# Local attention: order of maxima, exponentials and roots, the rotary halves in one operation, and the band mask on VectorE

## The chip, the cores and the metric

The kernel runs on one core of one Trainium2 chip. The metric is the device time of one launch in microseconds (us), as the median of several runs. Engines are named as in the profile: PE is TensorE (PEld its weight loads), DVE is VectorE, ACT is ScalarE, POOL is GpSimd, SP is SyncE.

## The reference, cut to what matters

The program is a four-layer decoder: each layer has an attention, a cross attention and a feed-forward part, each followed by a layer norm. Everything is f32, with a batch of 4 sequences of 512 tokens and a width of 128. The change lies in the feed-forward part of layer 1, which is itself a transformer of `DEPTH` = 6 blocks. Each block is a local attention and a gated feed-forward. Of the local attention, these lines of the reference tell what is computed (16 heads of 64, a window of 32):

```python
q = l2norm(q) * qs
k = l2norm(k) * ksc
...
q = q * cos * scale + rotate_half(q) * sin * scale
inv = 1.0 / scale
k = k * cos * inv + rotate_half(k) * sin * inv
out = local_attention(q, k, v)
...
mask = (it < jb) | (it > jb + w) | (jb == -1)
sim = jnp.einsum('bhwie,bhwje->bhwij', bq, bk2) * QK_SCALE
sim = jnp.where(mask, -jnp.finfo(sim.dtype).max, sim)
attn = jax.nn.softmax(sim, -1)
out = jnp.einsum('bhwij,bhwje->bhwie', attn, bv2)
```

`l2norm` divides a head's 64 values by the root of the sum of their squares; `rotate_half` swaps the two halves of 32 values of each head, with a sign. A query sees itself and the 32 keys before it. The kernel adds a band that is 0 where a key is seen and -1e30 elsewhere.

## The kernel before, in words

`local_transformer` (L2364) runs six blocks in a hardware loop; each calls `local_attention` (L1902) and then `gelu_ffn`. All weights of a block are loaded a block ahead.

`local_attention` cuts the 4 x 512 tokens into 16 tiles of 128 and each tile into four units of work, so G = 64. Each engine has its own program, all written over the same steps s = -7 ... 68, and each runs strictly in that order; semaphores tie them together. A step holds work of several ages:

- the query or key part of unit n = s + 7 (`LEAD`): PE projects 512 columns (L2010), ACT squares them (`local_squares`, L2092), DVE sums the squares of each head (`local_norm`, L2180), ACT makes the inverse roots by a logarithm and an exponential (L2114, L2117: "the roots"), and DVE multiplies the projection, still in its PSUM bank, by them into `local_raw` (L2190);
- POOL's rotary embedding of unit n (L2146 to L2152): `raw * cos`, the two swapped halves times `sin` in two operations, and their sum into `local_rot`;
- the transposition of unit s + 4 by PE (L2039), copied by ACT into `local_Q` or `local_K` (L2101, L2107);
- in two of four steps a value projection (L2046), copied out by DVE (L2202);
- the scores. PE makes those of two units at once, in the even steps (L2021, L2028), into three PSUM banks in turn. For each unit, DVE takes the row maxima (`local_negmax`, L2184), ACT the exponentials with their sums, four instructions (L2123), and DVE the reciprocal (L2205) and the probabilities (`local_probs`, L2208);
- of the unit before, PE's transposition of the probabilities (L2055) and ACT's copy of it (L2131); of the unit before that, PE's product with the values (L2068), copied out in even steps (L2167). Once in a tile PE does the output projection (L2077), and DVE adds it to the tokens (L2173).

The projections of queries, keys, values and output share **two PSUM banks**, used in turn in the order of `uses`: within the four steps of a tile qk0, v, qk1, v, qk2, qk3, out. PE waits before each projection until the one two places back has been read (`wait_for_bank`, L1992): for a query or key projection this is `scaled`, which L2190 raises. So qk1, qk2 and the next tile's qk0 each wait for the `local_raw` of the step before, and qk3 for a value copy.

The band mask is added by PE: before the scores of a pair, one matmul for each of the two banks multiplies a bf16 unit matrix with a bf16 band (`m.unit`, `m.bands`, L2020 to L2022), and the scores accumulate on it. `local_transformer` makes both tables once (L2383 to L2386).

The functions as they stand:

## Time and profile before

| what | value |
|---|---|
| median of 3 runs | 5413.22 us (5384.35 to 5419.07) |
| the profiled execution | 5386.55 us, its span 5384.8 us |
| busy share of the span | PE 84%, DVE 56%, ACT 54%, POOL 37% |
| POOL, rotary: L2149, L2146, L2152 | 557.6, 488.2 and 486.7 us busy |
| exponentials, L2123 | 474.2 us and 309.8 us for their sums |

The six passes of the local attention lie between 1262 and 3396 us. Each is a few us of start, a lead-in of seven steps in which only queries, keys and values are made, 64 steps with scores, and a drain. In the even part of a pass the pattern repeats from tile to tile, so that one tile tells what a pass costs. A share of busy time over the whole span says little here, since other stages have other limits.

### The profile page before, as it was taken

Reading aid. Unit: us, or ns where it says so; the run is one execution under the profiler, and the core shown is the slowest. Engines: PE = TensorE matmul, PEld = TensorE weight load, DVE = VectorE, ACT = ScalarE, POOL = GpSimd, SP = SyncE. Lnnn points to the kernel's source line nnn. Section 1 sums busy time; section 2 is a strip of 40 time slices with the busy share of each in tenths; the row PEclk is TensorE's granted clock in tenths of the full one; section 3 lists DMA queues with packets and bytes.
Section 4 is the critical chain, followed back from the end, with each engine's and each line's share of the span. In section 5 each row is a group of like instructions: output and inputs, shape, how many; then the busy total and the mean of one; then the engine's idle time right before and its main releaser. Section 6 shows DMA issues by size and latency. Waiting matters only on the chain. (4 is left out here: it accounts for less than half of the span.)

```text
span 5384.8 us, 98536 instructions
## 1 busy us (share of the span) xinstructions
PE 4535.6 (84%) x35524; PEld 2696.3 (50%) x35524; DVE 3041.0 (56%) x5774; ACT 2904.6 (54%) x8810; POOL 1985.9 (37%) x2126
## 2 busy tenths in 40 slices
PE   6998699997998979979889889855658988888999
PEld 2663355564654645646646556424445653223343
DVE  6551354455756747647557567359984554653333
ACT  4543334455756747747657577467764442553322
POOL 1320000236948939849569398013321310000000
PEclk8999789899999989999999999866669997996689
DMA  1000000001111111111111111100000000001000
GB/s 56 2 1 4 17 12 5 18 2 28 47 40 41 45 39 45 44 39 47 46 33 47 40 44 43 43 0 1 1 1 11 2 4 7 9 5 34 4 0 8
DMA packets 34474, 122.85 MB, mean 23 GB/s; under 512 B 8484, under 2 KB 9512, under 8 KB 32296
## 3 DMA queue, kind: packets, MB, share of 16 engines
q1 hardware_dynamic: 33960, 116.23, 8.0%
q8 instruction: 294, 4.82, 0.4%
q14 instruction: 220, 1.80, 0.1%
HBM read 37.24 MB, written 1.05 MB: 7 GB/s over the span
## 5 line engine op out<-in xcount | busy, mean ns | idle before, releaser
L706 POOL MEMSET norm_eps<- 128x1 f32 x16 | 1.6, 98 | 1596.4 <-POOLq L116 1551.9
L2149 POOL TENSOR_TENSOR local_other<-local_raw,local_sin 128x256 f32<-128x256 f32 x768 | 557.6, 726 | 60.2
L2010 PE MATMUL ps<-arena,local_xs 128*128 128x512 f32 x768 | 437.5, 654 | 111.2 <-DVE local_raw L2190 61.1
L2146 POOL TENSOR_TENSOR local_rot<-local_raw,local_cos 128x512 f32<-128x512 f32 x384 | 488.2, 1271 | 67.9 <-DVE local_raw L2190 67.9
L2152 POOL TENSOR_TENSOR local_rot<-local_rot,local_other 128x512 f32<-128x512 f32 x384 | 486.7, 1268 | 30.1
L2123 ACT ACTIVATE ps<-ps,local_negmax 128x96 f32<-128x96 f32 x1536 | 474.2, 309 | 41.5 <-DVE local_negmax L2184 41.4
L2190 DVE SCALAR_TENSOR_TENSOR local_raw<-local_inverse,ps 128x512 f32<-128x512 f32 x384 | 264.0, 687 | 278.3 <-ACT local_inverse L2117 278.3
L2180 DVE TENSOR_REDUCE local_norm<-local_squares 128x8 f32<-128x512 f32 x384 | 263.0, 685 | 129.5 <-ACT local_squares L2092 129.5
L2092 ACT ACTIVATE local_squares<-ps 128x512 f32<-128x512 f32 x384 | 229.8, 598 | 155.2 <-PE ps L2010 155.0
L2123 ACT ACTIVATION_READ_ACCUMULATOR ps<-ps,local_negmax 128x1 f32 x1536 | 309.8, 202 | 0.0
L2055 PE MATMUL ps<-const,local_probs 128*96 128x128 f32 x1536 | 239.7, 279 | 77.3 <-DVE local_probs L2208 77.3
L2039 PE MATMUL ps<-const,local_rot 128*128 128x128 f32 x1536 | 245.3, 282 | 50.5 <-POOL local_rot L2152 50.5
L2055 PEld LDWEIGHTS ps<-const,local_probs 128*96 128x96 f32 x1536 | 173.2, 127 | 194.2 <-DVE local_probs L2208 102.2
L2039 PEld LDWEIGHTS ps<-const,local_rot 128*128 128x128 f32 x1536 | 173.9, 141 | 191.8 <-POOL local_rot L2152 99.1
L2068 PE MATMUL ps<-local_pts,local_V_span 96*64 96x64 f32 x6144 | 266.9, 230 | 0.5
L2068 PEld LDWEIGHTS ps<-local_pts,local_V_span 96*64 96x64 f32 x6144 | 213.4, 139 | 72.2 <-issue 71.0
L2131 ACT COPY local_pts<-ps 96x512 f32<-96x512 f32 x384 | 221.4, 577 | 22.2 <-PE ps L2055 22.2
L2101 ACT ACTIVATE local_Q<-ps 128x512 f32<-128x512 f32 x192 | 114.6, 597 | 218.6 <-PE ps L2039 218.6
L1486 DVE TENSOR_REDUCE l3a_limits<-ps 128x1 f32<-128x512 f32 x256 | 165.0, 686 | 114.0 <-PE ps L1334 114.0
L2208 DVE TENSOR_TENSOR local_probs<-ps,local_total 128x384 f32<-128x384 f32 x384 | 214.1, 558 | 14.6 <-DVE local_total L2205 1.5
L2184 DVE TENSOR_REDUCE local_negmax<-ps 128x4 f32<-128x384 f32 x384 | 210.3, 548 | 7.0 <-PE ps L2028 7.0
L2010 PEld LDWEIGHTS ps<-arena,local_xs 128*128 128x128 f32 x768 | 120.0, 196 | 181.3 <-DVE local_raw L2190 104.1
(519 smaller groups left out, 10843.7 us busy)
## 6 DMA issues: line engine op xcount, KB each, us to landing
local_V_span<-local_V SPq DMA_DIRECT2D x96, 384.0 KB, 4.0
local_V_span<-local_V SPq DMA_DIRECT2D x96, 256.0 KB, 3.6
arena<-in_L1f_a SPq DMA_DIRECT2D x7, 2176.0 KB, 8.5
local_V_span<-local_V SPq DMA_DIRECT2D x72, 128.0 KB, 2.3
arena<-in_L3f SPq DMA_DIRECT2D x1, 3460.0 KB, 11.2
arena<-in_L1f_f SPq DMA_DIRECT2D x6, 537.5 KB, 3.9
arena<-in_L0f SPq DMA_DIRECT2D x1, 2824.5 KB, 9.7
arena<-in_L0x SPq DMA_DIRECT2D x1, 2049.5 KB, 9.3
```

Of the source, the lines that this page charges most:

```text
L2010: nc.tensor.matmul(bank("qk", n)[:, :], tokens_of(tile), w("Wqkv", QKV[i] * 512, (QKV[i] + 1) * 512), start=True, stop=True)\
L2039: mm = nc.tensor.transpose(TURN[:, c * P:(c + 1) * P], m.rot[:, n % 4, c * P:(c + 1) * P], core.ident)
L2055: mm = nc.tensor.transpose(PT[0:SPAN, u * P:(u + 1) * P], m.probs[:, g % 2, u, :], core.ident)
L2068: mm = nc.tensor.matmul(OUT[DH * h:DH * h + DH, c * SPAN_Q:(c + 1) * SPAN_Q], m.V_span[:, tile % 2, half_span, (2 * c + h) * DH:(2 * c + h ...
L2092: nc.scalar.activation(m.squares[:, n % 2, :], bank("qk", n)[:, :], ACT.Square).then_inc(squared, 1)
L2123: nc.scalar.activation(scores, scores, ACT.Exp, bias=m.negmax[:, s % 2, u:u + 1], accum_out=m.total[:, s % 2, u:u + 1])\
L2131: nc.scalar.copy(m.pts[:, g % 3, :, :].rearrange("p u q -> p (u q)"), PT[0:SPAN, :])\
L2146: link(nc.gpsimd.tensor_tensor(rot, raw, m.cos[:, t, a * DH:(a + 1) * DH].unsqueeze(1) .broadcast_to([P, 8, DH]), ALU.mult))
L2149: link(nc.gpsimd.tensor_tensor(other[:, :, lo:lo + HALF], raw[:, :, HALF - lo:DH - lo], m.sin[:, t, a * DH + lo:a * DH + lo + HALF].unsque ...
L2152: nc.gpsimd.tensor_tensor(rot, rot, other, ALU.add).then_inc(rotated, 1)
L2180: nc.vector.tensor_reduce(m.norm[:, n % 4, :], heads(m.squares[:, n % 2, :]), AX_X, ALU.add)\
L2190: nc.vector.scalar_tensor_tensor(out=heads(m.raw[:, n % 4, :]), in0=m.inverse[:, n % 4, :].unsqueeze(2).broadcast_to([P, 8, DH]), scalar=1 ...
```

## The change

Four things, all in the local attention:

- PE no longer adds the band. DVE adds it to the scores in their PSUM bank, one operation of 128 x 384 for each unit, and waits for it before the maxima. The two bf16 tables and their making go.
- On DVE, the maxima come ahead of the squares' sums, and the scaling into `local_raw` moves from before the exponentials' wait to the end of the step, behind the probabilities.
- On ACT, the four exponentials of a unit come ahead of the roots.
- On POOL, the two half-width products with `sin` become one of full width that reads the halves swapped.

```diff
@@ -1893,8 +1893,6 @@
         self.negmax, self.total = tmp("negmax", [P, 2, 4]), tmp("total", [P, 2, 4])
         self.probs, self.pts = tmp("probs", [P, 2, 4, SPAN]), tmp("pts", [SPAN, 3, 4, P])
         self.oT = tmp("oT", [P, 2, CHUNKS, TILE])
-        self.unit = tmp("unit", [P, P], BF16)
-        self.bands = tmp("bands", [P, 2, 4, SPAN], BF16)
         self.eps = tmp("eps", [P, 1])
         self.tiny = tmp("tiny", [P, 1])
 
@@ -1959,6 +1957,9 @@
 
     def heads(a):
         return a.rearrange("p (h d) -> p h d", d=DH)
+
+    def halves(a):
+        return a.rearrange("p (h j f) -> p h j f", j=2, f=HALF)
 
     with core.stage() as st:
         xs_low, xs_high = st.sem("xs_low"), st.sem("xs_high")
@@ -2016,10 +2017,6 @@
                     if s >= 2:
                         pe.wait_ge(probs_ready, s - 1)
                     first = tile % QT * TILE + SPAN_Q * half_span
-                    edge = int(tile % QT == 0 and half_span == 0)
-                    for i in range(2):
-                        nc.tensor.matmul(SC[(s + i) % 3][:, 0:UNITS * SPAN], m.unit[:, :],
-                                         m.bands[:, edge, :, :].rearrange("p u k -> p (u k)"), start=True, stop=False)
                     for u in range(UNITS):
                         for h in range(2):
                             for i in range(2):
@@ -2027,8 +2024,7 @@
                                 rows = slice(DH * h, DH * h + DH)
                                 mm = nc.tensor.matmul(SC[(s + i) % 3][rows_of(h, i), u * SPAN:(u + 1) * SPAN],
                                                       m.Q[rows, tile % 2, c, SPAN_Q * half_span:SPAN_Q * (half_span + 1)],
-                                                      m.K[rows, c, first:first + SPAN], start=False,
-                                                      stop=(u == UNITS - 1))
+                                                      m.K[rows, c, first:first + SPAN], start=True, stop=True)
                     mm.then_inc(scores_ready, 1)
                 n = s + LEAD - TURN_LAG
                 if 0 <= n < G:
@@ -2106,6 +2102,13 @@
                             act.wait_ge(scores_ready, 2 * (tile - 2))
                         nc.scalar.copy(m.K[:, c:c + 4, WINDOW + t * TILE:WINDOW + (t + 1) * TILE],
                                        TURN[:, :].rearrange("p (c q) -> p c q", c=4)).then_inc(flip_read, 1)
+                if 0 <= s < G:
+                    act.wait_ge(max_ready, s + 1)
+                    for u in range(UNITS):
+                        scores = SC[s % 3][:, u * SPAN:(u + 1) * SPAN]
+                        nc.scalar.activation(scores, scores, ACT.Exp, bias=m.negmax[:, s % 2, u:u + 1],
+                                             accum_out=m.total[:, s % 2, u:u + 1])\
+                          .then_inc(exp_ready, 1)
                 n = s + LEAD
                 if n < G:
                     act.wait_ge(summed, n + 1)
@@ -2116,13 +2119,6 @@
                     act.wait_ge(log_ready, n + 1)
                     nc.scalar.activation(m.inverse[:, n % 4, :], m.log[:, n % 4, :], ACT.Exp, scale=-0.5)\
                       .then_inc(inverted, 1)
-                if 0 <= s < G:
-                    act.wait_ge(max_ready, s + 1)
-                    for u in range(UNITS):
-                        scores = SC[s % 3][:, u * SPAN:(u + 1) * SPAN]
-                        nc.scalar.activation(scores, scores, ACT.Exp, bias=m.negmax[:, s % 2, u:u + 1],
-                                             accum_out=m.total[:, s % 2, u:u + 1])\
-                          .then_inc(exp_ready, 1)
                 g = s - 1
                 if 0 <= g < G:
                     act.wait_ge(turned, g + 1)
@@ -2145,10 +2141,9 @@
                     pool.wait_ge(flipped, n - 3)
                 link(nc.gpsimd.tensor_tensor(rot, raw, m.cos[:, t, a * DH:(a + 1) * DH].unsqueeze(1)
                                              .broadcast_to([P, 8, DH]), ALU.mult))
-                for lo in (0, HALF):
-                    link(nc.gpsimd.tensor_tensor(other[:, :, lo:lo + HALF], raw[:, :, HALF - lo:DH - lo],
-                                                 m.sin[:, t, a * DH + lo:a * DH + lo + HALF].unsqueeze(1)
-                                                 .broadcast_to([P, 8, HALF]), ALU.mult))
+                link(nc.gpsimd.tensor_tensor(halves(m.other[:, :]), halves(m.raw[:, n % 4, :])[:, :, ::-1, :],
+                                             m.sin[:, t, a * DH:(a + 1) * DH].rearrange("p (j f) -> p j f", f=HALF)
+                                             .unsqueeze(1).broadcast_to([P, 8, 2, HALF]), ALU.mult))
                 nc.gpsimd.tensor_tensor(rot, rot, other, ALU.add).then_inc(rotated, 1)
 
         @st.block.vector
@@ -2172,6 +2167,13 @@
                     dve.wait_ge(projected, tile + 1)
                     nc.vector.tensor_tensor(place_x, bank("out", tile)[:, 0:TILE], place_x, ALU.add)\
                       .then_inc(x_done, 1)
+                if 0 <= s < G:
+                    dve.wait_ge(scores_ready, s // 2 + 1)
+                    tile, half_span, _ = place(s)
+                    band = core.c("band_first" if tile % QT == 0 and half_span == 0 else "band")
+                    link(nc.vector.tensor_tensor(sc, sc, band.unsqueeze(1).broadcast_to([P, UNITS, SPAN]), ALU.add))
+                    nc.vector.tensor_reduce(m.negmax[:, s % 2, :], sc, AX_X, ALU.max, negate=True)\
+                      .then_inc(max_ready, 1)
                 n = s + LEAD
                 if n < G:
                     dve.wait_ge(squared, n + 1)
@@ -2179,18 +2181,6 @@
                         dve.wait_ge(inverted, n - 3)
                     nc.vector.tensor_reduce(m.norm[:, n % 4, :], heads(m.squares[:, n % 2, :]), AX_X, ALU.add)\
                       .then_inc(summed, 1)
-                if 0 <= s < G:
-                    dve.wait_ge(scores_ready, s // 2 + 1)
-                    nc.vector.tensor_reduce(m.negmax[:, s % 2, :], sc, AX_X, ALU.max, negate=True)\
-                      .then_inc(max_ready, 1)
-                if n < G:
-                    if n >= 4:
-                        dve.wait_ge(rotated, n - 3)
-                    dve.wait_ge(inverted, n + 1)
-                    nc.vector.scalar_tensor_tensor(out=heads(m.raw[:, n % 4, :]),
-                                                   in0=m.inverse[:, n % 4, :].unsqueeze(2).broadcast_to([P, 8, DH]),
-                                                   scalar=1e12, in1=heads(bank("qk", n)[:, :]), op0=ALU.min, op1=ALU.mult)\
-                      .then_inc(scaled, 1)
                 if values_at(s) is not None:
                     tile, i = values_at(s)
                     v = 2 * tile + i
@@ -2207,6 +2197,14 @@
                         dve.wait_ge(turned, s - 1)
                     nc.vector.tensor_tensor(m.probs[:, s % 2, :, :], sc, m.total[:, s % 2, :].unsqueeze(2)
                                             .broadcast_to([P, UNITS, SPAN]), ALU.mult).then_inc(probs_ready, 1)
+                if n < G:
+                    if n >= 4:
+                        dve.wait_ge(rotated, n - 3)
+                    dve.wait_ge(inverted, n + 1)
+                    nc.vector.scalar_tensor_tensor(out=heads(m.raw[:, n % 4, :]),
+                                                   in0=m.inverse[:, n % 4, :].unsqueeze(2).broadcast_to([P, 8, DH]),
+                                                   scalar=1e12, in1=heads(bank("qk", n)[:, :]), op0=ALU.min, op1=ALU.mult)\
+                      .then_inc(scaled, 1)
 
 
 def gelu_ffn(core, arena, m):
@@ -2380,10 +2378,6 @@
             @st.block.vector
             def _(dve):
                 nc.vector.tensor_copy(kept[:, :, :], core.tokens[:, :, PAD:PAD + S]).then_inc(copied, 1)
-                nc.vector.tensor_copy(bufs.unit[:, :], core.ident).then_inc(copied, 1)
-                for i, name in enumerate(("band", "band_first")):
-                    nc.vector.tensor_copy(bufs.bands[:, i, :, :], core.c(name).unsqueeze(1).broadcast_to([P, 4, SPAN]))\
-                      .then_inc(copied, 1)
 
             @st.block.gpsimd
             def _(pool):
```

What DVE issues in a step with a value copy, before. `local_norm` are the squares' sums, `local_negmax` the maxima, `local_raw` the scaled projection; the last row is the first of the next step:

```order
L2180 TENSOR_REDUCE local_norm<-local_squares 128x8
L2184 TENSOR_REDUCE local_negmax<-ps 128x4
L2190 SCALAR_TENSOR_TENSOR local_raw<-local_inverse,ps 128x512
L2202 COPY local_V<-ps 128x512
L2205 RECIPROCAL local_total<-local_total 128x4
L2208 TENSOR_TENSOR local_probs<-ps,local_total 128x384
L2167 COPY local_oT<-ps 128x8x64
```

The same step of DVE with the change (the lines are those of the changed kernel):

```order
L2174 TENSOR_TENSOR ps<-ps,const 128x384
L2175 TENSOR_REDUCE local_negmax<-ps 128x4
L2182 TENSOR_REDUCE local_norm<-local_squares 128x8
L2192 COPY local_V<-ps 128x512
L2195 RECIPROCAL local_total<-local_total 128x4
L2198 TENSOR_TENSOR local_probs<-ps,local_total 128x384
L2204 SCALAR_TENSOR_TENSOR local_raw<-local_inverse,ps 128x512
L2162 COPY local_oT<-ps 128x8x64
```

The band's sum is new at the head; the maxima passed the squares' sums; `local_raw` went from the third place to the last.

What ACT issues in the same step, before:

```order
L2092 ACTIVATE local_squares<-ps 128x512
L2107 COPY local_K<-ps 128x4x128
L2114 ACTIVATE local_log<-local_norm,local_tiny 128x8
L2117 ACTIVATE local_inverse<-local_log 128x8
L2123 ACTIVATE ps,local_total<-ps,local_negmax 128x96 x4
L2131 COPY local_pts<-ps 96x512
```

And with the change:

```order
L2088 ACTIVATE local_squares<-ps 128x512
L2103 COPY local_K<-ps 128x4x128
L2109 ACTIVATE ps,local_total<-ps,local_negmax 128x96 x4
L2117 ACTIVATE local_log<-local_norm,local_tiny 128x8
L2120 ACTIVATE local_inverse<-local_log 128x8
L2127 COPY local_pts<-ps 96x512
```

The exponentials passed the two instructions of the roots; the squares, which wait for PE's projection of the same step, still stand ahead of both.

## Rows read from the trace of the kernel before

**Rows 1.** Busy time by window: stretch, us, busy of each engine (instructions), PEclk, DMA, GB/s.
```profile
1849.70:1867.40 17.70, 16.62 (x194) 11.10 (x193) 12.69 (x26) 13.29 (x53) 15.89 (x16) 1.00 0.16 39
```
**Rows 2.** Waits of PE, whole span: who waited for whom, us, times, longest.
```profile
PE ps L2055 <- DVE local_probs L2208: 77.3, 94, 1.9
PE ps L2010 <- DVE local_raw L2190: 61.1, 104, 1.5
```
**Rows 3.** Timeline of one tile: start us, us, engine, line, operation [idle before].
```profile
1849.70 1.13 PE L2010 MATMUL ps<-arena,local_xs 128*128 128x512 f32 x2
...
1850.86 0.60 ACT L2092 ACTIVATE local_squares<-ps 128x512 f32<-128x512 f32 x1 [0.27 <-PE ps L2010]
...
1851.36 0.58 ACT L2107 COPY local_K<-ps 128x512 f32<-128x512 f32 x1
...
1852.85 0.69 DVE L2190 SCALAR_TENSOR_TENSOR local_raw<-local_inverse,ps 128x512 f32<-128x512 f32 x1 [0.21 <-ACT local_inverse L2117]
...
1853.60 1.13 PE L2010 MATMUL ps<-arena,local_xs 128*128 128x512 f32 x2 [0.42 <-DVE local_raw L2190]
...
1854.32 0.56 DVE L2208 TENSOR_TENSOR local_probs<-ps,local_total 128x384 f32<-128x384 f32 x1
...
1854.56 0.49 PE L2021 MATMUL ps<-local_bands,local_unit 128*128 128x384 bf16 x2
...
1854.79 0.68 DVE L2167 COPY local_oT<-ps 128x512 f32<-128x512 f32 x1
...
1854.98 0.89 PE L2028 MATMUL ps<-local_K,local_Q 64*64 64x96 f32 x32
...
1855.80 0.66 PE L2039 MATMUL ps<-const,local_rot 128*128 128x128 f32 x4
...
1856.49 0.60 ACT L2101 ACTIVATE local_Q<-ps 128x512 f32<-128x512 f32 x1 [1.14 <-PE ps L2039]
...
1856.98 0.29 ACT L2114 ACTIVATE local_log<-local_norm,local_tiny 128x8 f32<-128x8 f32 x1
1857.31 0.21 ACT L2117 ACTIVATE local_inverse<-local_log 128x8 f32<-128x8 f32 x1
1857.42 0.30 ACT L2123 ACTIVATE ps<-ps,local_negmax 128x96 f32<-128x96 f32 x1
...
1857.62 0.69 DVE L2190 SCALAR_TENSOR_TENSOR local_raw<-local_inverse,ps 128x512 f32<-128x512 f32 x1 [1.08 <-ACT local_inverse L2117]
...
1858.84 0.18 DVE L2205 RECIPROCAL local_total<-local_total 128x4 f32<-128x4 f32 x1 [0.53 <-ACT ps L2123]
...
1859.05 0.56 DVE L2208 TENSOR_TENSOR local_probs<-ps,local_total 128x384 f32<-128x384 f32 x1
...
1859.66 0.64 PE L2055 MATMUL ps<-const,local_probs 128*96 128x128 f32 x4 [0.66 <-DVE local_probs L2208]
...
1867.40 1.13 PE L2010 MATMUL ps<-arena,local_xs 128*128 128x512 f32 x2
```
**Rows 4.** Timeline in the drain of the same pass, where only the maxima are awaited.
```profile
1903.96 0.55 DVE L2184 TENSOR_REDUCE local_negmax<-ps 128x4 f32<-128x384 f32 x1
...
1904.54 0.32 ACT L2123 ACTIVATE ps<-ps,local_negmax 128x96 f32<-128x96 f32 x1 [0.36 <-DVE local_negmax L2184]
```
**Rows 5.** Costliest groups of the page: POOL's two products.
```profile
L2149 POOL TENSOR_TENSOR local_other<-local_raw,local_sin 128x256 f32<-128x256 f32 x768 | 557.6, 726 | 60.2
...
L2146 POOL TENSOR_TENSOR local_rot<-local_raw,local_cos 128x512 f32<-128x512 f32 x384 | 488.2, 1271 | 67.9 <-DVE local_raw L2190 67.9
```
**Rows 6.** Busy time by window, a lead-in and a drain: columns as in the first group.
```profile
1652.00:1656.00 4.00, 2.24 (x8) 0.99 (x8) 1.54 (x5) 2.28 (x11) 3.77 (x5) 1.00 0.01 2
...
1920.00:1924.00 4.00, 1.94 (x23) 1.57 (x24) 2.30 (x6) 2.03 (x10) 0.00 (x0) 0.91 0.00 0
1924.00:1928.00 4.00, 4.00 (x31) 3.52 (x30) 1.33 (x3) 1.68 (x9) 0.00 (x0) 0.50 0.01 4
```

## The prediction

> **What bounds the kernel now.** The change touches only the six passes of the local attention, so the busy shares of the whole span decide nothing. The first view is the busy time of one steady tile of four steps [rows 1]. It takes 17.70 us, in which PE is busy 16.62, POOL 15.89, ACT 13.29 and DVE 12.69. PE and POOL are nearly full, but neither is quite, so something ties them together. The second view, PE's waits [rows 2], names it: PE stood before the transposition of the probabilities 94 times (77.3 us), and before a query or key projection, waiting for DVE's `local_raw`, 104 times (61.1 us). The third view is the tile in order of time [rows 3], and there a loop closes.
>
> It begins with qk1 at 1849.70. ACT squares, DVE sums, ACT makes the roots, DVE scales at 1852.85; only then has qk2 a bank, at 1853.60: 3.90. From there PE reaches its transposition at 1855.80 (2.20), ACT copies Q at 1856.49 (0.69), makes the roots and starts the exponentials at 1857.42 (0.93), DVE takes the reciprocal at 1858.84 (1.42) and the probabilities at 1859.05 (0.21), and PE goes on at 1859.66 (0.61). PE then has work until the next tile's qk1 at 1867.40 (7.74). The sum is 17.70, the tile. So the time is that of a loop over four engines, not that of one of them. The reader is to see that two of its links are the very ones that the change reorders.
>
> **The change part by part.** The profiled execution took 5386.55 us, 0.5% under the median of 5413.22.
>
> *Scaling at the end of DVE's step.* This is the large term. Three of the four query and key projections of a tile (qk1, qk2, the next qk0) get their bank from the `local_raw` of the step before. Before, DVE did that as soon as the roots were there. Now it stands behind the probabilities, those behind the reciprocal, that behind the exponentials, and these on ACT behind the squares of the same step, which need PE's projection of that step. So from projection to projection, everything is in one row. The links, all [rows 3] unless named:
>
> - from `local_raw` to the projection that it frees 0.75 (1852.85 to 1853.60); from a projection to the squares 1.16 (1849.70 to 1850.86); squares to the copy behind them 0.50; copy to the next on ACT 0.49 (1856.49 to 1856.98); first exponential to reciprocal 1.42; reciprocal to probabilities 0.21; probabilities to the next on DVE 0.47 (1854.32 to 1854.79);
> - projection to scores 0.96 (to where the bands stood, 1853.60 to 1854.56); scores to DVE 0.92 (they last 0.89; 0.03 is what the squares need behind a projection's end); maxima to exponentials 0.58 [rows 4].
> - The band's sum on DVE has no row of its own. The nearest is the probabilities: as many elements, one operand in PSUM, 0.56. With the 0.03 by which the probabilities follow the reciprocal that they wait for, I take 0.59. As bounds: 0.47, the distance from one such operation to the next where nothing is awaited, and 0.69, an operation of 512 columns.
>
> *Step 0 of a tile, and step 2* (scores are made): 0.96 + 0.92 + 0.59 (band) + 0.58 + 1.42 + 0.21 + 0.47 + 0.75 = 5.90 from projection to projection. ACT's own way, squares and Q copy, is done earlier: the transposition comes at 0.96 + 0.82, the copy 0.69 later and ends 0.49 on, at 2.96, where the maxima let the exponentials go at 3.05.
>
> *Step 1* (no scores made; band and maxima are done while PE projects): 1.16 + 0.50 + 0.49 + 1.42 + 0.21 + 0.47 + 0.75 = 5.00.
>
> *Step 3*: qk3 itself does not wait for `local_raw`, but its exponentials wait for maxima, and DVE begins band and maxima of step 3 only behind the `local_raw` of step 2. That starts 5.90 - 0.75 = 5.15 after qk2. Then 0.60 (0.69 less the 0.09 by which DVE's next began early above), 0.59, 0.58, 1.42, 0.21, 0.47 and 0.75 follow: 9.77 from qk2 to the next qk0.
>
> The tile is then 5.90 + 5.00 + 9.77 = **20.67 instead of 17.70: 2.97 more**. The roots, now behind the exponentials, are in time in each step: 0.33 from logarithm to the second step and 0.31 from there to DVE, in all 0.64, against 0.21 + 0.47 for reciprocal and probabilities behind the same exponentials.
>
> *Exponentials and maxima ahead.* The gain is in the sum already: the 0.44 of the roots (1856.98 to 1857.42) no longer stand ahead of the exponentials. It is worth having where the probabilities are late, and is less than what the scaling loses.
>
> *Bands off PE.* 0.42 twice in a tile (1854.56 to 1854.98), also in the sum. *Band on DVE*: three times in the loop, 1.77.
>
> *Rotary halves.* Two products of 0.726 become one, which the full-width product prices at 1.271 [rows 5]; that saves 0.18 a step and one link. The bounds are a quarter more or less, since no row reads halves swapped in one operation. POOL's tile falls to some 15.2, and the loop of 20.67 covers it, also if the new form cost what the two did. So: nothing. *The three casts* run once, while POOL clears its tables: nothing.
>
> How often: `local_raw` is made in 57 of the 64 steps with scores, so 14 tiles of a pass carry the loop. In the lead-in POOL sets the pace and gains a little, in the drain the band's sum costs a little; I let these cancel. 2.97 x 14 x 6 = **249 us**, and 5386.55 + 249 = 5636. The median lies 27 above the profiled run; I put the forecast midway, at **5650 us**.
>
> Own bounds of this case: 13 to 16 tiles in the loop, 232 to 285; the band at 0.47 or 0.69, three times in 84 tiles, 30 less or 25 more; against the profiled run or the median, 0 or 27. From 5589 to 5724, and outward for links that I read from one tile.
>
> **Rivals.**
>
> *A, faster: throughput decides.* With seven steps of lead, `local_raw` could be late without harm. Then the fullest engine sets the tile: PE 16.62 - 0.84 = 15.8, POOL 15.2. That is 1.9 less a tile, 160 us in all, 5227. For it speaks that PE and POOL are above 89% busy in the tile. Against it, PE already waited 61.1 us for `local_raw` [rows 2], and in the tile it waits before qk2 as things are, 0.42 [rows 3], so that each delay of that `local_raw` reaches PE in full. A decides from the point where at most one of the three projections waits for its bank. Chance 6%. The Trainium skill, page Perfetto Trace Analysis, section Identifying the Most-Contended Engine, says to take the engine with the highest occupancy first; for PE it sets aside matmul busy time and looks at weight loads. By that rule POOL is the one, the change relieves it, and the kernel should gain. The trace disagrees: POOL too waited for DVE's `local_raw`, 67.9 us before its first product [rows 5].
>
> *B, no change.* Only step 1's surplus shows (5.00 against 3.90), and the others are swallowed by PE's own work, less 0.84 for the bands: 0.26 x 84 = 22 us, 5409. For it: part of a longer chain can hide behind PE's 16 us of work. Against it, the chains of steps 0 and 2 hold PE's projection and scores in the same row as DVE's and ACT's links, so they can't overlap. Chance 8%.
>
> *C, slower still: the clock.* PE would idle 20.67 - 15.8 = 4.9 us a tile, in three gaps of some 1.6. In the drain the granted clock fell from 1.00 to 0.50 (2.4 to 1.2 GHz) after a stretch with PE busy 1.94 of 4 us; in the lead-in it held at 1.00 with 2.24 of 4 [rows 6]. The changed tile has about 15.8 of 20.67, more than either. If it falls, the PE links double: 0.96 + 0.92 in steps 0 and 2, 1.16 in step 1, so 4.9 a tile. In a third of the tiles that is 137 more, 5790; in all 410, 6060. Chance 12%. The Trainium skill, page TensorE: Matmul & The Clock Gate, section A second HAM failure mode, tells of a kernel whose matmul groups, cycling through PSUM banks with short idles, made the clock swing between its levels; by it this rival would be the likely one. The lead-in's row speaks against that.
>
> **How the numbers follow.** Forecast 74%, A 6%, B 8%, C 12%. The range 5560 to 5760 takes the forecast's own bounds, widened by some 30 at either end, and the mild half of C. It leaves out A, B and the worse half of C. About 1% is what a measurement of this kernel can tell from no change; the runs shown spread by 0.65%. Faster by over 1%: A, 0.06. Within 1%: B, 0.08. Slower by over 1%: the rest, 0.86.
>
> **What would show it.** In the profile after, a steady tile of about 20.7 us, with PE waiting before three of four query and key projections for `local_raw`, 1.4 to 1.7 us each; steps of about 5.9, 5.0 and together 9.8; the exponentials waiting for maxima in even steps; POOL idle before its first product by 1 us a step and more. It is wrong if the tile is under 18.5, if the band's sum takes over 0.7, if the roots and not the probabilities end last before `local_raw`, or if the granted clock leaves 1.00 inside the steady tiles.

## The result, and the profile after

The changed kernel took 5734.47 us (median of 4 runs, 5724.96 to 5743.09), the kernel before 5398.78 (4 runs, 5378.83 to 5419.07): a ratio of 1.0623 [1.0593, 1.0654]. The profiled execution took 5724.96, 338 more than that of before.

The page after, columns as in the first pages. These are the groups that answer to [rows 2, 5], and the new band's sum:

```profile
L2011 PE MATMUL ps<-arena,local_xs 128*128 128x512 f32 x768 | 449.8, 671 | 422.4 <-DVE local_raw L2204 374.4
L2142 POOL TENSOR_TENSOR local_rot<-local_raw,local_cos 128x512 f32<-128x512 f32 x384 | 487.0, 1268 | 464.1 <-DVE local_raw L2204 464.1
...
L2144 POOL TENSOR_TENSOR local_other<-local_raw,local_sin 128x512 f32<-128x512 f32 x384 | 488.4, 1272 | 30.1
...
L2174 DVE TENSOR_TENSOR ps<-ps,const 128x384 f32<-128x384 f32 x384 | 215.7, 562 | 237.3 <-PE ps L2025 236.9
```

PE's wait for the scaling went from 61.1 us to 374.4, POOL's from 67.9 to 464.1. No new operation is dear: the band's sum takes 0.56, the single swapped product 1.27. DVE itself stands 237 us before the scores.

A steady tile after, by window (columns as in [rows 1]):

```profile
1506.88:1527.93 21.05, 16.26 (x189) 10.83 (x189) 14.83 (x30) 13.38 (x52) 15.21 (x13) 1.00 0.17 40
```

And the same tile in order of time, for [rows 3]; it begins with the projection of step 2:

```profile
1506.88 1.13 PE L2011 MATMUL ps<-arena,local_xs 128*128 128x512 f32 x2 [1.51 <-DVE local_raw L2204]
...
1510.09 0.32 ACT L2109 ACTIVATE ps<-ps,local_negmax 128x96 f32<-128x96 f32 x1
...
1512.21 0.68 DVE L2204 SCALAR_TENSOR_TENSOR local_raw<-local_inverse,ps 128x512 f32<-128x512 f32 x1
...
1512.80 0.56 DVE L2174 TENSOR_TENSOR ps<-ps,const 128x384 f32<-128x384 f32 x1
...
1513.39 0.56 DVE L2175 TENSOR_REDUCE local_negmax<-ps 128x4 f32<-128x384 f32 x1
...
1513.99 0.32 ACT L2109 ACTIVATE ps<-ps,local_negmax 128x96 f32<-128x96 f32 x1 [0.64 <-DVE local_negmax L2175]
...
1515.42 0.18 DVE L2195 RECIPROCAL local_total<-local_total 128x4 f32<-128x4 f32 x1 [0.87 <-ACT ps L2109]
1515.60 0.21 ACT L2120 ACTIVATE local_inverse<-local_log 128x8 f32<-128x8 f32 x1
1515.63 0.56 DVE L2198 TENSOR_TENSOR local_probs<-ps,local_total 128x384 f32<-128x384 f32 x1
...
1516.10 0.68 DVE L2204 SCALAR_TENSOR_TENSOR local_raw<-local_inverse,ps 128x512 f32<-128x512 f32 x1
...
1516.84 1.13 PE L2011 MATMUL ps<-arena,local_xs 128*128 128x512 f32 x2 [1.09 <-DVE local_raw L2204]
...
1517.89 0.89 PE L2025 MATMUL ps<-local_K,local_Q 64*64 64x96 f32 x32
...
1518.85 0.57 DVE L2174 TENSOR_TENSOR ps<-ps,const 128x384 f32<-128x384 f32 x1 [1.27 <-PE ps L2025]
...
1522.89 1.12 PE L2011 MATMUL ps<-arena,local_xs 128*128 128x512 f32 x2 [1.61 <-DVE local_raw L2204]
```

Step 0 runs from 1516.84 to 1522.89 (6.05), step 1 to 1527.88, where the next tile's projection stands in the same timeline (4.99), steps 2 and 3 together from 1506.88 to 1516.84 (9.96). The tile is 21.00 against 17.70. In each of the three waits PE stands for the `local_raw` just made.

Where the 338 us lie, between marks found in both traces (POOL's cosine table at a pass's start, DVE's sum into the tokens at a tile's end): 12 steady tiles in each pass 259.3 in all (236 from the 3.3 a tile, 23 from the clock, below); from a pass's start to its first finished tile 32.7; the last three tiles 20.2; between passes 8.6; ahead of the first pass -3.9. The other 21.6 lie in stages behind the attention, with unchanged code: nearly all in one that took 271 us before at a mean granted clock of 0.63 and 291 after at 0.57. One of the kernels below also had the shorter time there, the others the longer, and the runs of before differ among themselves by as much (5384 to 5420). I don't count it to the change. The same stages took 17.7 us more with the two orders alone and 22.9 more with band and rotary alone, so about that much of their loss is not theirs.

### The profile page after: what moved, and what is told of

Same layout as the page of the kernel before. It is cut to its first block and busy times, and to the rows that moved or that the text cites. A ratio compares the mean times of both kernels' runs of the same rounds, so it can differ in the third digit from the quotient of the medians.

```text
span 5723.2 us, 97765 instructions
## 1 busy us (share of the span) xinstructions
PE 4566.5 (80%) x35140; PEld 2716.8 (47%) x35140; DVE 3239.9 (57%) x6155; ACT 2916.8 (51%) x8810; POOL 1921.3 (34%) x1742
## 3 DMA queue, kind: packets, MB, share of 16 engines
HBM read 37.24 MB, written 1.05 MB: 7 GB/s over the span
## 5 line engine op out<-in xcount | busy, mean ns | idle before, releaser
L2011 PE MATMUL ps<-arena,local_xs 128*128 128x512 f32 x768 | 449.8, 671 | 422.4 <-DVE local_raw L2204 374.4
L2142 POOL TENSOR_TENSOR local_rot<-local_raw,local_cos 128x512 f32<-128x512 f32 x384 | 487.0, 1268 | 464.1 <-DVE local_raw L2204 464.1
L2144 POOL TENSOR_TENSOR local_other<-local_raw,local_sin 128x512 f32<-128x512 f32 x384 | 488.4, 1272 | 30.1
L2174 DVE TENSOR_TENSOR ps<-ps,const 128x384 f32<-128x384 f32 x384 | 215.7, 562 | 237.3 <-PE ps L2025 236.9
L2035 PE MATMUL ps<-const,local_rot 128*128 128x128 f32 x1536 | 258.4, 293 | 22.5 <-POOL local_rot L2147 22.2
L2035 PEld LDWEIGHTS ps<-const,local_rot 128*128 128x128 f32 x1536 | 185.9, 147 | 157.9 <-issue 78.6
L2042 PE MATMUL ps<-arena,local_xs 128*128 128x512 f32 x384 | 217.1, 649 | 9.8 <-DVE local_raw L2204 9.8
## 6 DMA issues: line engine op xcount, KB each, us to landing
arena<-in_L3f SPq DMA_DIRECT2D x1, 3460.0 KB, 10.9
```

The lines of the kernel that those rows point to most:

```text
L2011: nc.tensor.matmul(bank("qk", n)[:, :], tokens_of(tile), w("Wqkv", QKV[i] * 512, (QKV[i] + 1) * 512), start=True, stop=True)\
L2035: mm = nc.tensor.transpose(TURN[:, c * P:(c + 1) * P], m.rot[:, n % 4, c * P:(c + 1) * P], core.ident)
L2142: link(nc.gpsimd.tensor_tensor(rot, raw, m.cos[:, t, a * DH:(a + 1) * DH].unsqueeze(1) .broadcast_to([P, 8, DH]), ALU.mult))
L2144: link(nc.gpsimd.tensor_tensor(halves(m.other[:, :]), halves(m.raw[:, n % 4, :])[:, :, ::-1, :], m.sin[:, t, a * DH:(a + 1) * DH].rearrang ...
```

## The experiments

The twelve steady tiles of the second pass in each kernel's trace, by window (columns as in [rows 1]); which kernel it is stands ahead of each.

Before:

```profile
1686.32:1899.09 212.77, 199.52 (x2306) 133.27 (x2305) 152.33 (x302) 159.41 (x624) 195.11 (x197) 1.00 0.18 44
```

After:

```profile
1743.41:1998.15 254.74, 199.53 (x2257) 131.97 (x2256) 177.06 (x350) 161.35 (x624) 182.28 (x145) 0.98 0.15 37
```

The two orders alone:

```profile
1738.13:1987.48 249.35, 202.24 (x2305) 134.06 (x2304) 151.31 (x301) 158.08 (x624) 190.98 (x193) 1.00 0.16 38
```

Band and rotary alone:

```profile
1697.33:1910.81 213.48, 191.58 (x2268) 128.48 (x2263) 176.20 (x350) 163.23 (x625) 185.73 (x147) 1.00 0.18 44
```

The exponentials' order alone:

```profile
1780.91:2063.92 283.01, 220.06 (x2306) 142.81 (x2304) 150.17 (x301) 159.21 (x624) 191.19 (x193) 0.93 0.14 33
```

The scaling's place alone:

```profile
1787.25:2075.56 288.31, 215.56 (x2305) 140.12 (x2304) 151.02 (x301) 159.72 (x624) 190.98 (x193) 0.95 0.13 33
```

A third bank, in the changed kernel:

```profile
1699.76:1920.55 220.79, 198.49 (x2257) 124.48 (x2256) 174.11 (x350) 164.60 (x624) 184.22 (x147) 1.00 0.17 43
```

A third bank, in the kernel before:

```profile
1701.42:1923.51 222.09, 203.56 (x2305) 128.87 (x2304) 152.21 (x301) 160.12 (x624) 194.94 (x198) 1.00 0.17 43
```

The scaling put back in the changed kernel:

```profile
1757.23:2014.30 257.07, 200.80 (x2260) 134.35 (x2264) 175.15 (x349) 161.88 (x624) 182.87 (x145) 0.97 0.15 37
```

The new orders in step 2 only:

```profile
1681.60:1891.07 209.47, 199.06 (x2305) 133.24 (x2304) 152.20 (x302) 159.86 (x625) 183.93 (x146) 1.00 0.18 45
```

The maxima's place alone:

```profile
1693.08:1909.25 216.17, 199.41 (x2306) 133.17 (x2304) 151.79 (x301) 161.33 (x625) 194.85 (x197) 1.00 0.18 44
```

One rotary product alone:

```profile
1685.42:1898.15 212.73, 199.41 (x2306) 133.24 (x2305) 152.45 (x302) 159.69 (x624) 185.96 (x148) 1.00 0.18 44
```

The number behind each stretch is the one to read: a twelfth of it is the mean tile of that pass. (A tile named below is the middle one of the 72 steady tiles of the six passes; where the clock made tiles longer, the shortest.) From kernel to kernel ACT's busy time stays between 158 and 165 us, POOL's between 182 and 195 and PE's between 192 and 220, while the length goes from 209 to 288. So none of these engines' own work sets it.

**The two orders alone.** The kernel before, with these moves and nothing else (here and below, where no code is quoted, a name stands for an operation with its waits):

```diff
 # ACT, a step
+exponentials (wait max_ready)
 log, inverse (wait summed)
-exponentials (wait max_ready)
 # DVE, a step
+maxima
 squares' sums
-maxima
-scaling (local_raw)
 value copy; reciprocal, probabilities
+scaling (local_raw)
```

> The kernel before with nothing but the change's two new orders: on ACT the exponentials ahead of the roots, on DVE the maxima first and the scaling last. The bands stay on PE, the rotary products stay two. Theory (the orders, through the two banks that the projections wait for): the steps of the changed tile, 6.05, 4.99 and 9.96 us, less the band's sum on DVE (0.57, three times in the loop), plus the bands on PE (0.42, twice), give 20.1 us a tile against 17.7; 2.4 x 84 tiles is some 205 us, and with what the change itself lost outside its steady tiles, up to 340: a ratio of 1.04 to 1.063. Rival (the band's sum on DVE and DVE's load are the loss): without them the tile falls back towards 17.7, a ratio of 0.99 to 1.015.

Ratio 1.0516 [1.0491, 1.0541]; tile 20.75. The orders carry most of the loss; the rival is out. The tile is 0.65 above the expected 20.1: in steps 0 and 2 the exponentials here wait for ACT's copy of Q, whose transposition PE does behind bands and scores. In one step 0 they start 3.38 us after the projection, where the change with the band on DVE has 3.20. So the band's place is worth 0.25 a tile between these two kernels, not the 0.9 of the sum.

**Band and rotary alone**, on the orders of before:

```diff
-matmul(unit, bands), start=True; scores start=False
+matmul(scores), start=True
+DVE: sc = sc + band, ahead of the maxima
-POOL: two half-width products
+POOL: one, halves swapped by the view
```

> The other half: the band added by DVE, no casts, one rotary product, and the orders of before on both engines. Theory (the orders): DVE has 2.25 us more in a tile of 17.7 that it fills to 12.69, and PE 0.84 less; in the loop the 0.42 of the bands goes, and the band's 0.57 stands only before exponentials that wait for the roots anyway. The tile stays at 17.3 to 17.9, a ratio of 0.99 to 1.005. Rival (band and DVE's load): steps 0 and 2 each grow by some 0.57 and DVE's queue delays the scaling, 1.1 to 1.7 us a tile, 95 to 140 us, a ratio of 1.018 to 1.026.

Ratio 1.0103 [1.0086, 1.012], between the two expectations. The steady tile is 17.75, as the theory said. Most of what it missed in the attention lies in the drain: the last three tiles of the six passes take 237.4 us together against 208.8. There steps follow one another over DVE and ACT alone. A step of before, from probabilities to probabilities:

```profile
1916.78 0.56 DVE L2208 TENSOR_TENSOR local_probs<-ps,local_total 128x384 f32<-128x384 f32 x1
1917.25 0.55 DVE L2184 TENSOR_REDUCE local_negmax<-ps 128x4 f32<-128x384 f32 x1
...
1919.47 0.56 DVE L2208 TENSOR_TENSOR local_probs<-ps,local_total 128x384 f32<-128x384 f32 x1
```

and one of this kernel:

```profile
1914.43 0.56 DVE L2206 TENSOR_TENSOR local_probs<-ps,local_total 128x384 f32<-128x384 f32 x1
...
1914.90 0.56 DVE L2181 TENSOR_TENSOR ps<-ps,const 128x384 f32<-128x384 f32 x1
...
1915.49 0.56 DVE L2182 TENSOR_REDUCE local_negmax<-ps 128x4 f32<-128x384 f32 x1
...
1917.73 0.56 DVE L2206 TENSOR_TENSOR local_probs<-ps,local_total 128x384 f32<-128x384 f32 x1
```

2.69 against 3.30: in the drain each band's sum counts in full. The drains are 28.6 us of the 66.0 between the two profiles; 10.9 lie between the passes, 4.2 in the steady tiles, and 22.9 in the unchanged stages behind the attention. So 1.0% is too much for this half. Without those stages the halves are 257 and 43 us, together 300 of the change's 317; the lower clock that cost the change 23 us in its steady tiles shows in those of neither half.

**The exponentials' order alone**: of the first diff only ACT's part.

> One order alone: ACT's exponentials ahead of the roots; DVE keeps its order, with the scaling ahead of the probabilities. Theory (the scaling is late because its roots are late, wherever DVE has it): from projection to projection 1.16 to the squares, 0.63 to their sums, 0.60 to the maxima, 0.58 to the exponentials, 1.26 for these, 0.64 for the roots, 0.75 to the freed projection: 5.6 in steps 0, 1 and 2, and 4.9 + 0.6 + 0.7 + 0.6 + 0.6 + 1.3 + 0.6 + 0.75 = 10 for steps 2 and 3 together. A tile of 21.3 or more, 300 us or more, a ratio of 1.055 to 1.08: as slow as the whole change, or slower. Rival (what I put first in the prediction: the scaling's place at the end of DVE's step is the loss): with the scaling back in its place the exponentials ahead bring 0.44 in a step, a ratio of 0.98 to 1.01.

Ratio 1.0864 [1.0843, 1.0886]; the shortest tile 22.14, 62 of the 72 steady ones longer by over 0.3. Worse than the whole change, and the scaling's place was that of before. The maxima's too: here they stand behind the squares' sums, which wait for this step's projection.

**The scaling's place alone**: of the first diff only the two rows of `local_raw`.

> The other order alone: DVE's scaling at the end of its step, behind the probabilities; ACT keeps the roots ahead of the exponentials, DVE the squares' sums ahead of the maxima. Theory (whatever puts the scaling behind this step's exponentials closes the loop): 1.16 to the squares, 0.63 to their sums, 0.72 to the roots, 0.44 to the exponentials, 1.42 to the reciprocal, 0.21, 0.47 and 0.75: 5.8 in steps 0, 1 and 2, and 9.7 for steps 2 and 3 together; 21.3 us a tile or more, a ratio of 1.055 to 1.09. Rival (the exponentials ahead on ACT are the loss, the scaling's place is none): the roots are as early as before, and DVE waits 0.5 for the reciprocal at most; a ratio of 1.00 to 1.02.

Ratio 1.0964 [1.0922, 1.1006]; the shortest tile 23.04. The rival is out as well: either order is enough. Each leaves the scaling behind this step's exponentials, here by DVE's order, above through late roots. My sums by links (21.3) were 0.8 and 1.7 short.

**A third bank, in the changed kernel:**

```diff
-SC, PT, OUT, TURN = core.ps[0:3], core.ps[3], core.ps[4], core.ps[6]
+SC, PT, OUT, TURN = core.ps[0:3], core.ps[3], core.ps[4], core.ps[3]
 ...
-    return core.ps[5 + 2 * (use_at[kind, i] % 2)]
+    return core.ps[5 + use_at[kind, i] % 3]
 ...
-    k = use_at[kind, i] - 2
+    k = use_at[kind, i] - 3
 ...
+    # rows' transposition: pe.wait_ge(pts_ready, s - 1)
+    # probabilities': pe.wait_ge(flip_read, min(G, s + LEAD - TURN_LAG + 1))
```

> The changed kernel with three PSUM banks in turn for the projections instead of two. The third is gained by letting the two transpositions (the rotated rows and the probabilities) share one bank; for that PE waits before each for ACT's copy out of the other. No order changes. Theory (the loss is the wait of qk1, qk2 and qk0 for the scaling of the step just before, because they alternate between two banks): with three banks a projection waits for a scaling or copy one use earlier, the loop opens, and the tile falls from 21.0 to what PE (15.8), POOL (15.2) and the shared bank allow, 16.5 to 18.5 us; 2.5 to 4.5 less in 84 tiles is 210 to 380, a ratio to the kernel before of 0.99 to 1.03. Rival (ACT's and DVE's orders are slow in themselves: exponentials that wait for maxima, sums that wait behind them): the banks change nothing and the shared one costs, 21 us a tile or more, 1.06 to 1.08.

Ratio 1.0115 [1.007, 1.016]; tile 18.38, orders untouched. PE's waits in the attention now:

```profile
PE ps L2037 <- POOL local_rot L2150: 76.8, 106, 3.0
...
PE ps L2054 <- ACT local_Q L2100: 70.1, 90, 0.8
PE ps L2054 <- ACT local_K L2106: 69.0, 90, 0.8
...
PE ps L2054 <- DVE local_probs L2201: 33.2, 17, 2.5
```

The wait for `local_raw`, 374.4 us after the change, is no longer among them; the shared bank's (ACT's copies) took 139 of its place. So it was the bank that turned a late scaling into lost time.

**A third bank, in the kernel before**: the same edit.

> The control of the run before: the same three banks and the same shared one in the kernel before. There local_raw held qk2 up by 0.42 in a tile, which the third bank gives back; the shared bank adds a wait for ACT's copy of the probabilities, which stands last in ACT's step. Theory: 17.3 to 18.5 us a tile, a ratio of 0.98 to 1.015; with it the orders of before are no longer worth 3 us a tile, and the two three-bank kernels come within 1.5% of each other. Rival (the orders are slow in themselves): this one stays near 1.00 and the changed one 5% or more above it.

Ratio 1.0153 [1.0138, 1.0169]; tile 18.51. With three banks the orders of before and of the change differ by 0.13 a tile, where with two it was 3.3. PE waits 139 us for the shared bank in this kernel too, so a small difference between the orders could hide behind that wait; but 2.6 of the 3.3 went with the bank alone. The bank costs before more than it gives (17.70 to 18.51).

**The scaling put back in the changed kernel:**

```diff
 maxima; squares' sums
+scaling (local_raw)
 value copy; reciprocal, probabilities
-scaling (local_raw)
```

> The changed kernel with DVE's scaling put back ahead of the value copy and the probabilities; the maxima stay first, and ACT keeps the exponentials ahead of the roots. Theory (behind these exponentials the roots are late, so DVE's place for the scaling is none of the cost): the scaling waits 0.64 for the roots where it waited for reciprocal and probabilities (0.21 + 0.47), the probabilities then come behind it; step 0 5.9 to 6.1, a tile of 20.5 to 21.3, a ratio of 1.05 to 1.07. Rival (the scaling's place at the end is the loss, as the prediction named it): the tile falls to 18.8 or less, a ratio under 1.025.

Ratio 1.0644 [1.0627, 1.066], tile 21.13: nothing is won. This run speaks against the prediction's wording, below. It also tells why the exponentials' order alone (22.14) was worse than all the moves together: this kernel differs from that one by the maxima in front, and by band and rotary. Step 1 of a tile with the exponentials' order alone, from squares' sums to scaling:

```profile
1530.47 0.69 DVE L2180 TENSOR_REDUCE local_norm<-local_squares 128x8 f32<-128x512 f32 x1 [0.64 <-ACT local_squares L2092]
...
1531.08 0.55 DVE L2184 TENSOR_REDUCE local_negmax<-ps 128x4 f32<-128x384 f32 x1
...
1531.66 0.32 ACT L2113 ACTIVATE ps<-ps,local_negmax 128x96 f32<-128x96 f32 x1 [0.74 <-DVE local_negmax L2184]
...
1533.59 0.69 DVE L2190 SCALAR_TENSOR_TENSOR local_raw<-local_inverse,ps 128x512 f32<-128x512 f32 x1 [1.96 <-ACT local_inverse L2124]
```

and step 1 here:

```profile
1805.97 0.56 DVE L2175 TENSOR_REDUCE local_negmax<-ps 128x4 f32<-128x384 f32 x1
...
1806.44 0.68 DVE L2182 TENSOR_REDUCE local_norm<-local_squares 128x8 f32<-128x512 f32 x1
...
1806.56 0.32 ACT L2109 ACTIVATE ps<-ps,local_negmax 128x96 f32<-128x96 f32 x1
...
1808.48 0.69 DVE L2188 SCALAR_TENSOR_TENSOR local_raw<-local_inverse,ps 128x512 f32<-128x512 f32 x1 [1.37 <-ACT local_inverse L2120]
```

With the maxima behind the sums, the exponentials wait 0.74 for them, and with the exponentials the roots and the scaling; with the maxima in front they don't wait.

**The new orders in step 2 only**, with one rotary product and the bands on PE:

```diff
+if s % 4 == 2: exponentials
 log, inverse
-exponentials
+if s % 4 != 2: exponentials
 # DVE: maxima first, scaling last if s % 4 == 2, else as before
```

> The kernel before with one rotary product, and the change's orders on ACT and DVE only in the third of a tile's four steps, whose projection's successor (qk3) waits for a value copy and not for the scaling; the bands stay on PE. Theory (a late scaling costs only where a projection waits for it): the exponentials of that step come up to 0.44 earlier, the probabilities with them, nothing else waits; 0.2 to 0.4 less a tile, 17 to 35 us, a ratio of 0.992 to 0.998. Rival (each use of the new orders costs, in that step by what the late scaling takes from the next step's sums and maxima): 0.3 to 1.5 more a tile, a ratio of 1.005 to 1.025.

Ratio 0.9931 [0.9917, 0.9945], 5373.86 us; tile 17.44. It beats both kernels, if by less than 1%; how much of that is the rotary product's, the last run tells.

**The maxima's place alone**: of the first diff DVE's two rows of the maxima.

> The kernel before with one move alone: on DVE the maxima ahead of the squares' sums. Roots stay ahead of the exponentials, the scaling ahead of the probabilities. Theory (the maxima's place only delays the sums in the two steps that make scores: 0.96 + 0.42 + 0.92 from the projection to the maxima, 0.60 for these, where the sums could start at 1.79; 1.1 later in steps 0 and 2, of which step 2's frees no projection and PE's work covers part): 0.3 to 1.1 more a tile, a ratio of 1.004 to 1.018. Rival (the maxima ahead carry a third or more of the loss): above 1.02.

Ratio 1.0043 [1.0029, 1.0057], tile 18.00: the small end of the theory.

**One rotary product alone.**

> The kernel before with the two half-width rotary products in one, and nothing else. Theory (POOL is covered by the loop in the steady tiles): 17.70 a tile as before; only the lead-in, where POOL sets the pace over some seven steps, gains 0.18 to 0.2 a step, 1 to 2 us a pass, 6 to 12 in all: a ratio of 0.997 to 1.000. Rival (this, and not the new order in one step, is what the run with the new orders in the third step gained): 0.992 to 0.996.

Ratio 0.9958 [0.9945, 0.9971]. The steady tile stays (17.71), as the theory said, but the gain is over its range and in the rival's: 12.0 us lie in the lead-ins, and 15.0 in the last three tiles of the passes, which I had not thought of. There the last but one output projection takes 2.05 us in each pass, where before it took 2.70 to 3.79 with the clock at its lower level for part or all of it; that is about half of the 15. (The two profiles are of one length, 5386.0 and 5384.8: between the passes 8.1 go back, and before had the shorter time in the unchanged stages. The ratio is that of the medians.) So the larger part of what the new orders in step 2 seemed to gain is the rotary product's. Left for the order itself are 0.27%, with intervals that just touch; the tiles show it more plainly, twelve of them 3.3 us shorter, 20 in all.

## Why the prediction was right, and where it was not

*The loop.* Right, link by link: step 0 6.05 (5.90 forecast), step 1 4.99 (5.00), steps 2 and 3 9.96 (9.77). What the forecast lacked in the tile, 0.33, sits for the most part in two links: from projection to scores 1.05, where I had 0.96 from a row with the bands in that place, and from scores to DVE 0.96, where I had 0.92. Both stand in step 0 and again ahead of the `local_raw` of step 2, 0.27 in all; the rest are hundredths in other links. The measured time is 85 above the forecast, inside the range.

*The large term's name.* Wrong. I put the loss to the scaling at the end of DVE's step. With it put back, the kernel stays where it was (1.0644); with it alone moved, it is worse than the whole change. The cause is that a step's scaling stands behind its exponentials, and ACT's order does that as well as DVE's. The 0.64 for the late roots, which I took as "in time", was the second lock on the same door. All three moves together cost less (1.0516) than the exponentials' or the scaling's alone (1.0864, 1.0964). With exponentials and maxima in front the scaling's place hardly matters (21.13 and 21.00 a tile), and without the maxima in front the tile is 22.14: the maxima's move gives back about 1 us, though alone it costs 0.3. (The kernels of this comparison differ by band and rotary too, which between others were worth 0.05 to 0.25 a tile.) The scaling last with the maxima in front and the roots early was not run, so why that one alone is the worst stays open.

*A, throughput.* Out. POOL was relieved, and its idle time grew; its one product alone leaves the tile at 17.71. The Trainium skill's rule in Perfetto Trace Analysis, Identifying the Most-Contended Engine, would have had a gain here; in the steady tile the runs disagree, and the 0.4% of the one product lies outside it.

*B, no change.* Out: the surplus of steps 0 and 2 came in full.

*C, the clock.* Came true in part, and with it one of the prediction's own signs of being wrong, a granted clock that leaves 1.00 inside the steady tiles. A third of the tiles have it, as C's mild half said, but at a sixth of its price, 23 us for 137, since the lower clock lasts for a part of the tile only. 25 of the 72 are longer than 21.0 by 0.7 to 1.2. One in the first pass, by stretches of 2 us, PE's busy time first and the granted clock after POOL's:

```profile
1372.00:1374.00 2.00, 0.73 (x18) 0.55 (x16) 1.69 (x5) 1.75 (x9) 0.30 (x1) 1.00 0.00 0
1374.00:1376.00 2.00, 1.66 (x6) 1.14 (x7) 1.32 (x3) 0.50 (x1) 1.56 (x2) 0.84 0.00 0
1376.00:1378.00 2.00, 2.00 (x5) 0.83 (x4) 0.69 (x1) 1.75 (x9) 1.92 (x2) 0.50 0.00 0
1378.00:1380.00 2.00, 1.49 (x21) 0.97 (x19) 1.91 (x5) 1.21 (x5) 0.33 (x1) 0.81 0.01 4
```

Right behind one of the gaps the clock is at its lower level (1.2 GHz) for some 3 us. With the orders alone, bands on PE, no steady tile is longer than 20.94 (the mean clock is 1.00 above); the two single orders have a mean clock of 0.93 and 0.95. That is a part of what makes them so slow, not all: their shortest tiles are 22.14 and 23.04. The Trainium skill, page TensorE: Matmul & The Clock Gate, section A second HAM failure mode, tells of such swings; the trace agrees, with 25 of 72 tiles.

*Lead-in and drain cancel.* Wrong, though small: band and rotary together lose 29 us in the drains and win 2 in the lead-ins.

*The casts, nothing.* Right: they were worth 0.45 us, once. From the start of POOL's clears to the first pass's tables it took 7.03 before and 6.58 after. (The rest of the 3.9 by which the first pass begins earlier was there before the clears: they started at 1255.77 before, at 1252.36 after.)

*Signs.* The waits before three projections: 1.51, 1.09, 1.61 (1.4 to 1.7 forecast, so one falls short). POOL before its first product: over 1 us in three of four steps. The exponentials wait for maxima only in step 3 (0.64); in steps 0 and 2 ACT's Q copy ends at the same moment as the maxima. "Roots end last": no, in step 3 their last operation is done at 1515.81, and the scaling starts behind the probabilities at 1516.10.

*Size.* 249 forecast against 317 without the stage behind the attention: 28 of the 68 are the 0.33 a tile (84 tiles), 23 the clock, the rest the two ends of a pass and what lies between passes.

## What to carry to other kernels

When engines share a ring of two buffers, follow what frees a buffer from one use to the next. An operation that frees one should not stand, on any engine of its chain, behind other long work of its step: here the next projection then waited for maxima and exponentials that it does not need. Where nothing waits for the buffer (here step 2, whose successor waits for something else) the same order can win. Move the parts of a change one at a time, and in pairs: here two of three moves cost more alone than all three together.

## What the runs showed of the hardware

The same 128x128 cast from f32 to bf16 on DVE takes 0.59 us in one other stage of this kernel and 0.23 in a third, and took 3.61 beside a clear by POOL:

```profile
1256.02 4.59 POOL L2392 MEMSET local_V_span<- 96x4096 f32 x1
1257.08 3.61 DVE L2383 CAST local_unit<-const 128x128 bf16<-128x128 f32 x1
1257.21 3.95 DVE L2385 CAST local_bands<-const 128x384 bf16<-128x384 f32 x2
```
```profile
L1706 DVE CAST l1a_unit<-const 128x128 bf16<-128x128 f32 x1 | 0.6, 593 | 0.0
```

The clear ends at 1260.61, the first cast at 1260.69. POOL's clear took 4.59 before and after, with and without the casts. With a third bank in the changed kernel, without casts, DVE's copy that starts just ahead of the clear (`local_kept`) took 4.80 where it takes 1.35 in every other run, and the clear 3.51. That it is the clear that holds DVE up was not tried by itself.
